# Four chained attention layers on one core: the last layer's output four steps later, and its image branch cut up anew among VectorE's steps

## The reference

```python
q, k, v = heads(x @ Wq), heads(text @ Wk), heads(text @ Wv)
x = merge(softmax(q k^T * scale) v) @ Wout + bout + x
```

```python
qsem = l2norm(probs_text @ text_ehs)
fused = q k_ip^T * scale + 0.5 * (qsem . l2norm(ip_ehs))
ip_out = (softmax(fused) * spatial_mask) v_ip
```

## Time and profile before

| | us |
|---|---|
| median of 3 runs | 2118.23 (2114.12 to 2127.46) |
| the profiled execution | 2120.95 |
| its span, first to last instruction | 2119.2 |
| PE busy in it | 1995.2 (94%) |
| DVE busy in it | 1477.4 (70%) |
| ACT busy in it | 1121.0 (53%) |

### The profile page before, as it was taken

One profiled execution on the slowest core, in us unless ns is written; L12 is line 12 of the kernel. 1 busy time (PEld: TensorE's weight loads), 2 busy tenths in 40 slices (PEclk: granted clock), 3 DMA queues, 4 the chain that ended last, 5 costly groups with the idle time before them and its releaser, 6 DMA issues.

```text
span 2119.2 us, 71731 instructions
## 1 busy us (share of the span) xinstructions
PE 1995.2 (94%) x27866; PEld 1685.1 (80%) x27866; DVE 1477.4 (70%) x4462; ACT 1121.0 (53%) x2979; POOL 425.3 (20%) x744
## 2 busy tenths in 40 slices
PE   5899999999999999999999999999999999999975
PEld 4788888888888888888887888888888888888754
DVE  3367777777776676777777767777776777777763
ACT  1355555555555455555555555555555555555531
POOL 1122122122212112212212212122221221222110
PEclk9999999999999999999999999999999999999985
DMA  4211211211211121121121121111212112111100
GB/s 120 58 39 49 57 48 44 59 48 44 57 55 45 49 50 49 50 53 52 44 58 48 44 58 48 46 55 50 51 48 57 49 44 58 48 49 37 27 13 6
DMA packets 117679, 103.93 MB, mean 49 GB/s; under 512 B 45304, under 2 KB 94112, under 8 KB 117344
## 3 DMA queue, kind: packets, MB, share of 16 engines
q1 hardware_dynamic: 115424, 98.25, 17.2%
q10 hardware_dynamic: 1920, 1.09, 0.3%
HBM read 34.13 MB, written 5.41 MB: 19 GB/s over the span
## 4 chain that ended last, share of the span: by engine, by line
PE 68%; SPq 11%; DVE 11%; issue 5%; DMA 3%; ACT 1%; ACTq 0%; POOL 0%; DVEq 0%; POOLq 0%
PE ps_s L815 11%; PE ps_s L779 9%; PE ps_c L839 8%; SPq L601 6%; PE ps_c L906 5%; PE ps_k L859 5%; PE ps_k L706 4%; PE ps_k L864 4%; PE ps_q L758 4%; PE ps_k L681 3%; PE ps_c L895 3%; DVE top L1177 3%; SPq L584 3%; PE ps_c L872 3%; DMA q_sb<-top_t 3%
## 5 line engine op out<-in xcount | busy, mean ns | idle before, releaser
L1058 ACT ACTIVATE p_t<-ps_s 116x512 f32<-116x512 f32 (+1 forms) x1024 | 501.4, 544 | 102.6 <-PE ps_s L815 97.5
L1177 DVE TENSOR_REDUCE top<-ps_s 128x6 f32<-128x462 f32 (+3 forms) x1024 | 510.6, 543 | 33.6 <-PE ps_s L779 32.8
L1393 POOL TENSOR_TENSOR k_blocks<-k_sb,mask_k 128x231 f32<-128x231 f32 x384 | 212.0, 574 | 642.5 <-PE ps_s L815 620.8
L779 PE MATMUL ps_s<-k_blocks,q_sb 32*128 32x231 f32 (+1 forms) x3584 | 337.5, 376 | 2.8 <-ACT p_t L1058 2.3
L815 PE MATMUL ps_s<-q_sb,k_blocks 32*116 32x128 f32 (+1 forms) x7168 | 297.6, 285 | 16.9 <-DMA q_sb<-top_t 14.8
L815 PEld LDWEIGHTS ps_s<-q_sb,k_blocks 32*116 32x116 f32 (+1 forms) x7168 | 245.9, 177 | 57.3 <-issue 29.8
L839 PE MATMUL ps_c<-p_t,v_rows 116*27 116x128 f32 (+1 forms) x7168 | 281.3, 279 | 6.9 <-ACT p_t L1058 6.9
L1217 DVE TENSOR_TENSOR weighted<-ps_k,probs 128x462 f32<-128x462 f32 (+1 forms) x256 | 142.1, 555 | 186.8 <-PE ps_k L864 185.0
L779 PEld LDWEIGHTS ps_s<-k_blocks,q_sb 32*128 32x128 f32 x3584 | 231.4, 185 | 47.4 <-issue 8.2
L839 PEld LDWEIGHTS ps_c<-p_t,v_rows 116*27 116x27 f32 (+1 forms) x7168 | 209.8, 107 | 42.3 <-issue 19.8
L1086 ACT ACTIVATE o_t<-ps_c 128x256 f32<-128x256 f32 x256 | 98.1, 383 | 261.7 <-PE ps_c L895 196.7
(11 more groups left out here) (118 smaller groups left out, 3403.5 us busy)
## 6 DMA issues: line engine op xcount, KB each, us to landing
v_rows<-v_img SPq DMA_DIRECT2D x128, 227.4 KB
context<-in_ctx SPq DMA_DIRECT2D x64, 336.0 KB, 3.1
q_sb<-top_t SPq DMA_DIRECT2D x984, 7.0 KB
v_rows<-v_img SPq DMA_DIRECT2D x64, 115.2 KB
v_rows<-v_img SPq DMA_DIRECT2D x64, 112.2 KB
v_rep<-v_dram SPq DMA_DIRECT2D x64, 50.0 KB
gram<-g_img SPq DMA_DIRECT2D x64, 46.3 KB
x_in<-in_x SPq DMA_DIRECT2D x64, 40.0 KB, 1.9
```

The lines of the kernel that those rows point to most:

```text
L779: ins = pe.matmul(ps_s[:, z * 512 + j * GT:z * 512 + j * GT + n], q_sb[c % 3][lo:lo + QUAD, j * S:(j + 1) * S], k_blocks[c % 3][lo:lo + QU ...
L1058: act.activation(to, source, ACT.Exp, scale=SCALE).then_inc(p_ready, 1)
L1177: dve.tensor_reduce(top_at(c, z), s.rearrange("p (h t) -> p h t", t=T)[:, :, 0:n], AX.X, ALU.max).then_inc(s_top, 1)
L1393: pool.tensor_tensor(k_blocks[c % 3][:, j * GT:(j + 1) * GT].rearrange("p (h t) -> p h t", t=T), keys_of(l, b // 2)[:, at:at + T].unsqueez ...
```

## The change

1. **Output of the last layer.** It moves from 7 steps behind its scores to 11 (two constants: `out_step` and `T_END`). The kind of the step stays 2. As the results `o_last` and the masked values `v_ip` now live longer, `o_last` gets a third buffer, and POOL's `mask_values` waits for the output three batches earlier before it writes `v_ip`.
2. **Image steps 12 to 18** go from the end of step c + 5 (kind 0) to the front of step c + 7 (kind 2), ahead of `weigh`.
3. **The exponential, image steps 19 and 20 and the weights** go from c + 6 (kind 1) to c + 8 (kind 3), at the same place within the step.

```diff
@@ -63,7 +63,7 @@
-T_END = L * (B - 1) + (L + 1) * (L - 1) + LAG + 4
+T_END = L * (B - 1) + (L + 1) * (L - 1) + LAG + 8
@@ -142,7 +142,7 @@
 def out_step(t):
-    return t - LAG if layer(t - LAG) != L - 1 else t - LAG - 4
+    return t - LAG if layer(t - LAG) != L - 1 else t - LAG - 8
@@ -302,7 +302,7 @@
-        o_last = [sb(f"o_last{i}", [128, 3 * TRI * D]) for i in range(2)]
+        o_last = [sb(f"o_last{i}", [128, 3 * TRI * D]) for i in range(3)]
@@ -890,7 +890,7 @@
-                o = o_last[c // 4 % 2] if final else o_sb[c % 2]
+                o = o_last[c // 4 % 3] if final else o_sb[c % 2]
@@ -1095,8 +1095,8 @@
                 if exists(t + 1):
                     queries(k, t + 1)
-                if ip(t - 6):
-                    image_exp(k, t - 6)
+                if ip(t - 8):
+                    image_exp(k, t - 8)
@@ -1232,7 +1232,7 @@
-                to = o_last[c // 4 % 2] if ip(c) else o_sb[c % 2]
+                to = o_last[c // 4 % 3] if ip(c) else o_sb[c % 2]
@@ -1343,9 +1343,11 @@
                 if added(t):
                     add_top(k, t)
-                if ip(t - 6):
-                    image_branch(k, t - 6, 19, 21)
-                    image_weights(k, t - 6)
+                if ip(t - 8):
+                    image_branch(k, t - 8, 19, 21)
+                    image_weights(k, t - 8)
+                if ip(t - 7):
+                    image_branch(k, t - 7, 12, 19)
                 if e_waves(t):
                     weigh(k, t, 0)
@@ -1363,8 +1365,6 @@
                 if e_waves(t):
                     weigh(k, t, 1)
-                if ip(t - 5):
-                    image_branch(k, t - 5, 12, 19)
                 if e_gram(t):
                     image(k, t)
@@ -1421,6 +1421,8 @@
                 if k is None:
                     pool.wait_ge(ld_w, N_LD)
+                if b >= NX:
+                    pool.wait_ge(ot_psum, raised(k, out, 4 * (b - NX) + (L + 1) * (L - 1) + LAG + 8))
                 pool.tensor_tensor(v_ip[b % NX][:, :], v_rep[b % NX][:, :], mask_vip[:, :], ALU.mult)\
```

## The result

Over 20 runs of each, interleaved, the changed kernel takes 2111.77 us (2099.58 to 2123.41) and the one before 2122.02 (2114.12 to 2132.09). The ratio is 0.9941, with a 95% interval of 0.9922 to 0.996: 4 to 8 per mille off, or 8 to 17 us. I had forecast 16.4 us off, and 2102 us within 2086 to 2117. The median lies in the range, 10 us over the forecast: 3.8 of these because the kernel before takes 2122.0 us over 20 runs and not the 2118.2 of the three that I started from, the other 6.2 because less was gained.

The account below looks back on a forecast made before the run. PE, busy 94%, was held at L825 by DVE's row maxima, then at L815 by their DMAs behind SP's queue. Terms -15.5 - 1.3 + 0.4 = -16.4 us took 2118.2 to 2101.8, rounded 2102; range 2086 to 2117.

Parts of the forecast that it names:

- The wait of L825, 0.77 us a round: PE's wait in kind 1 for row maxima from DVE; moving image steps 12 to 18 removes all 0.77 us.
- The landing takes a part of it: At L815 in kind 1, the maxima's DMAs land at SP's own time, limiting the gain to 15.5 us.
- My sum of rooms: Room before L815 over 59 rounds: 23 with none, 27 averaging 0.32 us, 9 gaining 0.77; sum 15.5 us.
- L815's waits: PE's waits in kind 1 for the maxima's DMAs, to grow from 14.8 to some 45 us.
- Rival B: SP's queue gives way and the landing follows PE: nearly all 0.77 a round, 46 us, 2072; half, 2095 to 2085; chance 0.20.
- Kinds 2 and 3 at price 0: Moved image work fits DVE's idle time: 1.69 us before `weigh` in kind 2, 0.79 in kind 3; no cost.
- Step 22, 1.3 us: One output leaves step 22 in PE's list for the end, shortening the step from 7.99 us; gain 1.3 us.
- The end, 0.4 us: Second last output runs beside the last image branch; its new x between image steps 18 and 19 costs 0.4 us.
- Rival C, the clock: Longer waits at L815 in kind 1 drop PE's clock to half; ten further falls give 2134 us; chance 0.06.
- The total: Whole kernel: -15.5 - 1.3 + 0.4 = -16.4 us, median forecast 2101.8, rounded 2102, 0.8% less.

Follow-up runs that it names:

- the same lag: Kernel before, output still seven steps behind its scores, no third buffer, image steps 12 to 18 in kind 1 behind the row maxima: 2098.24 us, ratio 0.9897.
- second and third of after: The changed kernel run again without edit, for a second and third profile: 2107.16 us (ratio 0.9917) and 2102.94 us in its one run.

## Why the prediction was right, point by point

- **The wait of L825, 0.77 us a round.** Right. It went where said, and the two kernels with the other queue order measure it by itself: 0.81.
- **The landing takes a part of it.** Right, and it was the term that decided: 0.4 us a round is what came. My sum of rooms, 15.5 us over 59 rounds, is 14.2 for the 54 of the middle; measured were 20.9. The term was too small by a third of what was measured. I had taken the landing as fixed to kind 3's scores. By the semaphore updates it lay 20.34 us behind them before (mean of two profiles, 54 rounds each) and 20.21 after (mean of three), so it came 0.13 us earlier, up to 7 us in all. That is the size of the miss, and it fits L815's waits, which came to 39.5 us and not 45. Rival B had this direction and was too large. In seven profiles it goes with the later output: with only the output later it was 20.26, with the same lag 20.35, so the four with the later output lie between 20.20 and 20.26 and the three without between 20.32 and 20.37. By what path the output does this is open.
- **Kinds 2 and 3 at price 0.** Right: the steps of kind 3 add up to 484.98 us before and after, those of kind 2 to 432.1 and 431.2 (first profile of each).
- **Step 22, 1.3 us.** Right to the hundredth: 7.99 to 6.67.
- **The end, 0.4 us.** Right for the place that was named, and incomplete for the end as a whole. The new x of the second last output does stand between image steps 18 and 19, as these rows of the changed kernel show:

```profile
2098.23 0.24 DVE L1301 TENSOR_TENSOR f_sub<-fused,f_top 128x80 f32<-128x80 f32 x1
2098.67 0.35 DVE L1328 SCALAR_TENSOR_TENSOR x_out<-ps_c,bias,x_work 128x128 f32<-128x128 f32 x1 [0.20 <-PE ps_c L911]
2099.04 0.36 DVE L1330 SCALAR_TENSOR_TENSOR x_out<-ps_c,bias,x_work 32x128 f32<-32x128 f32 x1
2099.42 0.24 DVE L1304 TENSOR_REDUCE f_sum<-f_exp 128x20 f32<-128x80 f32 x1
```

  From L1301 to L1304 it is 1.19 us; before, L1304 began 0.40 us after its engine fell idle, some 0.65 us after L1301. So 0.54 us is the price there. From the first scores of the last step to the end it is 46.8 us in both profiles of before and 47.3 in the second and third of after, so this price is all that the last step shows. The end as a whole is 1.4 to 3 us longer in these two, so 0.8 to 2.5 us lie ahead of the last step, in a stretch that held 4 and 8 us more at 1.2 GHz. That this is the clock fits the numbers; it was not tried.
- **Rival C, the clock.** It came true, but at another place than I named. In the middle the changed kernel's waits at L815 do not let the clock fall more often than before. At the end, where PE waits anyway, one profile of three had 98 us at 1.2 GHz within the last 170, the others 64 and 68, and the kernel before 60 and 60. It took 11 to 12.5 us of the 22 that the middle of the first profile had gained, which is why span and middle tell different stories. By the mean clocks above, more than half of the changed kernel's executions had so low a clock. I had given this rival 0.06, from the one fall in the middle of one profile; the half-speed stretches at the end did not enter its price.
- **The total.** -20.9 in the middle, -1.3 in step 22, +1.0 in the twelve steps between middle and end (92.0 us before, 93.1 after, on average) and +1.4 to +3 at the end make -18 to -20 us. Executions of like clock differ by 16.4 and 18.2 us. The two measurements over all executions say -12.5 (8 to 17) and -17.6 (12 to 24): the first has 13 of its 20 changed executions at 0.974 or less; the clocks of its 20 executions of the kernel before are not on record. So the forecast of 16.4 us came as near as it did by two misses of opposite sign, a landing term 6.7 us too small and a low clock that was left out of the sum. That part is luck.

## What to carry to other kernels

Before you take a wait away, look at what the same instruction, or the next one on that engine, waits for by another path, and read the room round by round: here two paths of nearly equal length ended at one step, each removal alone gave 21 and 13 us in the profiles, and both 49. Once the first was made, one swap of two lines on the DMA queue brought the other 28: urgent small moves ahead of bulk ones that are not waited for so soon. And check a profile's gain in the steady middle apart from its end: the spans of two executions of the same kernel differed by 8 us, their ends by 12.5, their middles by 1.5 the other way. The medians do not leave the clock out, so put executions of like granted clock side by side as well.

## What the runs showed of the hardware

- The granted clock's falls are scattered, and they stand at long waits. The same program had one, one and two falls in the middle in three profiles of the changed kernel, one and four in two of the kernel before, and the last 160 us or so of these held between 60 and 98 us at 1.2 GHz. In the middles of all twelve profiles there are 17 falls. Each began within 1.5 us of the end of a wait of L815 of 0.71 to 2.66 us, one of the six longest of its profile. No fall in these middles stands elsewhere, and most of the waits had none. What the Trainium skill describes of waits for DMAs ("TensorE: Matmul & The Clock Gate", section "HAM oscillation — how this bites in real kernels") was seen in single rounds here, never time after time, although L815 waited in 47 to 49 places.
- A small VectorE instruction beside GpSimd's `fold` (L1402) took 1.13 us, nearly four times its usual 0.30. From the second profile of the changed kernel, near its end:

```profile
2087.46 1.44 POOL L1402 TENSOR_TENSOR weighted<-weighted 128x720 f32<-128x720 f32 x1 [27.34 <-DVE weighted L1217]
2087.87 1.13 DVE L1314 SCALAR_TENSOR_TENSOR p_ip<-f_exp,fside,f_rec 128x80 f32<-128x80 f32 x1
```

  The Trainium skill, "GPSIMD Engine Reference", section "Specifications", lists this: GpSimd shares its SBUF interfaces with VectorE and contends with instructions of two SBUF inputs. The trace agrees for this one, in all three profiles of the changed kernel; in the middle of the run the moved steps met no GpSimd work. An image step that did not move (L1280) meets one there once a round, in both kernels, and takes 0.45 us there instead of 0.18.
- A move of 7 KB occupies SP's queue about as long as a placement of 227 KB: 0.78 and 0.82 us in the median of the kernel before. Four moves take 3.7 us above, four placements 3.3. So what counts here is its place in the queue and not its bytes.
